# Local transformer: order of the turns and projections within a step

## The reference

```python
def attn_layer(x, Wqkv, qs, ksc, Wo):
    qkv = x @ Wqkv
    q, k, v = (sh(t) for t in jnp.split(qkv, 3, -1))      # 16 heads of 64
    q = l2norm(q) * qs
    k = l2norm(k) * ksc
    q = q * cos * scale + rotate_half(q) * sin * scale
    k = k * cos * inv + rotate_half(k) * sin * inv
    out = local_attention(q, k, v)                         # softmax in windows
    return out.transpose(0, 2, 1, 3).reshape(b, n, INNER) @ Wo
...
for i in range(DEPTH):                                     # DEPTH = 6
    x = attn_layer(shift_tokens(x), Wqkv[i], q_scale[i], k_scale[i], Wo[i]) + x
    x = ffn_layer(shift_tokens(x), ln_g[i], ln_b[i], W1[i], b1[i], W2[i], b2[i]) + x
```

## Time and profile before

| | |
|---|---|
| median of three timed runs | 2600.63 us (2596.15 to 2601.51) |
| the profiled execution | 2589.45 us, span 2587.7 us |
| PE busy | 2448.3 us (95%), 52349 matmuls |
| DVE busy | 2154.9 us (83%) |
| ACT busy | 2033.9 us (79%) |
| POOL busy | 1519.4 us (59%) |

### The profile page before, as it was taken

One profiled execution on the slowest core, in us unless ns is written; L12 is line 12 of the kernel. 1 busy time (PEld: TensorE's weight loads), 2 busy tenths in 40 slices (PEclk: granted clock), 3 DMA queues, 4 the chain that ended last, 5 costly groups with the idle time before them and its releaser, 6 DMA issues. The chain is left out here.

```text
span 2587.7 us, 118567 instructions
## 1 busy us (share of the span) xinstructions
PE 2448.3 (95%) x52349; PEld 1973.1 (76%) x52349; DVE 2154.9 (83%) x2455; ACT 2033.9 (79%) x4077; POOL 1519.4 (59%) x1029
## 2 busy tenths in 40 slices
PE   6799999999999999999999999699999999997999
PEld 2488888888888888888888887467776776775787
DVE  5888888888888888888888886389898988885898
ACT  4689888898889899898998886667676766664776
POOL 3788888888888888887898784122222222222110
PEclk9899999999999999999999999799999999999999
DMA  3234433443444344334443332123232322221221
GB/s 99 56 93 95 108 78 93 94 110 83 97 94 110 83 96 99 95 85 98 103 100 82 86 83 59 45 46 69 45 73 48 67 47 66 51 58 30 83 74 41
DMA packets 275793, 202.01 MB, mean 78 GB/s; under 512 B 117568, under 2 KB 215880, under 8 KB 274248
## 3 DMA queue, kind: packets, MB, share of 16 engines
q1 hardware_dynamic: 275280, 194.42, 31.3%
HBM read 36.96 MB, written 1.11 MB: 15 GB/s over the span
## 5 line engine op out<-in xcount | busy, mean ns | idle before, releaser
L514 POOL TENSOR_TENSOR lt_t_sin<-lt_qk,lt_tab 128x512 f32<-128x512 f32 x384 | 683.3, 1801 | 222.2 <-DVE lt_qk L1298 220.1
L519 POOL TENSOR_TENSOR lt_qr<-lt_qr,lt_t_sin 128x1024 f32<-128x1024 f32 x192 | 457.7, 2384 | 28.2 <-POOL lt_t_sin L514 0.9
L2082 DVE TENSOR_REDUCE fa_neg_max<-bank 128x1 f32<-128x1024 f32 x256 | 301.6, 1220 | 91.2 <-PE bank L1879 89.7
L2004 ACT ACTIVATE fa_prob<-bank,fa_neg_max 128x1024 f32<-128x1024 f32 x128 | 142.6, 1114 | 216.5 <-DVE fa_neg_max L2082 164.2
L1905 PE MATMUL bank<-fa_prob_t,fa_v 32*64 32x128 f32 x16384 | 293.6, 276 | 16.5 <-issue 11.8
L1905 PEld LDWEIGHTS bank<-fa_prob_t,fa_v 32*64 32x64 f32 x16384 | 244.4, 130 | 78.0 <-issue 58.1
L2092 DVE STREAM_TRANSPOSE fa_prob_t<-fa_prob 128x1024 f32<-128x1024 f32 x256 | 302.1, 1219 | 0.0
L607 PE MATMUL bank<-lt_w_high,lt_x_high 128*128 128x512 f32 x576 | 262.3, 455 | 0.8 <-ACT lt_v_tok L1011 0.4
L979 ACT COPY lt_qk<-bank 128x512 f32<-128x512 f32 x384 | 224.3, 589 | 23.7 <-PE bank L609 2.8
L1298 DVE TENSOR_TENSOR lt_qk<-lt_qk,lt_rn 128x2048 f32<-128x2048 f32 x96 | 239.8, 2498 | 2.4 <-ACT lt_rn L1005 2.2
L1291 DVE TENSOR_REDUCE lt_ssq<-lt_qr 128x32 f32<-128x2048 f32 x96 | 218.9, 2280 | 25.6 <-ACT lt_qr L987 25.6
(11 more groups left out here) (260 smaller groups left out, 5853.1 us busy)
## 6 DMA issues: line engine op xcount, KB each, us to landing
lt_v<-lt_v_tok SPq DMA_DIRECT2D x576, 128.0 KB
fa_v<-fa_v_tok SPq DMA_DIRECT2D x256, 128.0 KB, 2.7
lt_v<-lt_v_tok SPq DMA_DIRECT2D x192, 64.0 KB
lt_k_t<-lt_k_t SPq DMA_DIRECT2D x84, 128.0 KB, 2.9
lt_v<-lt_v SPq DMA_DIRECT2D x168, 64.0 KB, 2.0
lt_w_raw<-in_lt_wqkv_dram SPq DMA_DIRECT2D x36, 256.0 KB, 3.6
ex_cw_all<-cw_kept SPq DMA_DIRECT2D x8, 1024.0 KB, 4.6
lt_x_s<-h_in SPq DMA_DIRECT2D x96, 64.0 KB, 2.7
```

What stands on the lines that cost most here:

```text
L514: pool.tensor_tensor(dst[:, :, i, :], src[:, :, 1 - i, :], tab[:, g // 2 % 2, 1, at:at + 32].unsqueeze(1).to_broadcast([P, HEADS, 32]), AL ...
L519: pool.tensor_tensor(qr[:, g % 2, half], qr[:, g % 2, half], t_sin[:, :], ALU.add).then_inc(S.rotated, 1)
L2082: dve.tensor_reduce(neg_max[:, u % 2, par:par + 1], bank[:, 2 * par:2 * par + 2, :].rearrange("p a n -> p (a n)"), AX.X, ALU.max, negate=T ...
```

## The change

On TensorE, and in the same way in the order of the banks and in ScalarE's emptying:

- before: query turns (j 0, 1), two projections, key turns (j 2, 3), two projections, variance (odd steps), attention's turn, scores;
- after: query turns, variance (odd steps), attention's turn, key turns, four projections, scores.

```diff
@@ order of the banks
                 for j in (2 * a, 2 * a + 1):
                     if live(i):
                         uses["turn", i, j] = len(uses)
-                for j in (2 * a, 2 * a + 1):
-                    if live(i + 2):
-                        uses["qk", i + 2, j] = len(uses)
-            if live(i - 2):
-                uses["att", i - 2, 0] = len(uses)
-                uses["att", i - 2, 1] = len(uses)
+                if live(i - 2) and a == 0:
+                    uses["att", i - 2, 0] = len(uses)
+                    uses["att", i - 2, 1] = len(uses)
+            for j in range(4):
+                if live(i + 2):
+                    uses["qk", i + 2, j] = len(uses)
@@ TensorE
                         for j in (2 * a, 2 * a + 1):
                             if live(i):
                                 turn_qk(i, j)
-                        for j in (2 * a, 2 * a + 1):
-                            if live(i + 2):
-                                project_qk(i + 2, j)
-                        if i == 0 and a == 0:
+                        if live(i - 2) and a == 0:
+                            if even(i, 5) is not None:
+                                variance(even(i, 5))
+                            turn_att(i - 2, 0)
+                            turn_att(i - 2, 1)
+                    if even(i, 5) is not None and not live(i - 2):
+                        variance(even(i, 5))
+                    for j in range(4):
+                        if live(i + 2):
+                            project_qk(i + 2, j)
+                        if i == 0 and j == 1:
                             second_var(3)
-                    if even(i, 5) is not None:
-                        variance(even(i, 5))
-                    if live(i - 2):
-                        turn_att(i - 2, 0)
-                        turn_att(i - 2, 1)
@@ ScalarE
                         for j in (2 * a, 2 * a + 1):
                             if live(i):
                                 empty_turned(i, j)
-                        for j in (2 * a, 2 * a + 1):
-                            if live(i + 2):
-                                empty_qk(i + 2, j)
-                        if i == 0 and a == 0:
+                        if live(i - 2) and a == 0:
+                            empty_att(i - 2, 0)
+                            empty_att(i - 2, 1)
+                    for j in range(4):
+                        if live(i + 2):
+                            empty_qk(i + 2, j)
+                        if i == 0 and j == 1:
                             second_log(3)
                             second_rstd(3)
-                    if live(i - 2):
-                        empty_att(i - 2, 0)
-                        empty_att(i - 2, 1)
```

## The result

The changed kernel takes 2612.86 us (median of 7 runs, 2608.98 to 2619.65). The kernel before, run beside it, takes 2597.98 us (7 runs, 2595.04 to 2601.51). The ratio is 1.006 [1.0048, 1.0073]: slower by 14.9 us.

The account below looks back on a forecast made before the run. TensorE's own instruction stream was taken to set the step length in the local transformer. The terms 11.3 + 6.9 - 3.5 = 14.7 gave +15 us, so 2616 us, range 2600 to 2628.

Parts of the forecast that it names:

- The reordering itself at nothing: TensorE in the local transformer: no instruction added or removed, a block costs the same wherever it stands; cost 0.
- the lead-in: Extra time before the mask matmul, now behind a projection: 0.10 us a step kept, bounds 0 and 0.20.
- "faster" rival: Before the mask and scores: lead-in (9.3 us) and late instructions (13) both go, giving -4, so 2596; chance 0.10.
- Part 1, down step: Attention's turn waits for VectorE's second norm_att half; scores 0.31 us late, 0.24 a step on average, 47 steps: 11.3 us.
- The guess for steps without the split: Down steps without ScalarE's weight split (0.52 us): exponent still comes last, barely; where not, the whole 0.31 us counts.
- Part 2, up step: Variance waits 0.10 us for ScalarE's square; scores 0.14 late, nothing absorbs it; 46 x 0.15 = 6.9 us.
- Banks: Four rotating banks emptied by ScalarE's copies in time for turns and projections; tightest margin 0.4 us, cost nil.
- Part 3, late instructions: Fewer late instructions in the scores: 3.5 us off 8.4 us of standing matmuls; bounds 0 and -13.
- the rule of proportion: Ahead of the scores, six matmuls instead of ten cross 4 in 10 fewer packet boundaries, hence 3.5 us off.
- the clock: Longer transpose runs drop TensorE's clock for the twelve projections behind: 12 x 0.24 x 93 = 268, so 2884; chance 0.03.
- "Nothing": VectorE and ScalarE run ahead once TensorE is slower, the waits close: 2601, within 0.2%; chance 0.05.
- The draw by supply: Slow projections ahead of the scores relieve late instructions by 13 us instead of 3.5: +5, so 2606; chance 0.20.

Follow-up runs that it names:

- `down_only`: New order in even (down) steps alone, old order in odd ones, against the kernel before: 2608.64 us, ratio 1.0042.
- `swap_after`: Whole new order, plus both halves of VectorE's norm_att ahead of the residual in odd steps, against the kernel before: 2593.35 us, ratio 0.9978.
- `up_only`: New order in odd (up) steps alone, old order in even ones, against the kernel before: 2600.09 us, ratio 1.0009.
- `mid`: Attention's turn and variance moved only ahead of the second pair of projections, against the kernel before: 2587.33 us, ratio 0.9953.
- `both_after`: `swap_after` plus TensorE's centring ahead of weigh_v and ScalarE's square earlier in even steps, against the kernel before: 2597.2 us, ratio 0.999.
- `fill_old`: New order only from step 4 on, old order in the steps that fill the pipeline, against the kernel before: 2610.0 us, ratio 1.0036.

## Why the prediction was right

The forecast was 2616.0 for a median of 2612.86, and +15 for +14.9 us. The agreement of the sum is closer than that of its terms.

**The reordering itself at nothing, and the lead-in.** Right. The last L609 starts at 737.06 and the mask at 737.38: 0.32 where projections are 0.23 apart, so the lead-in of about 0.10 stays behind a projection. With it half of the "faster" rival falls. The late instructions, its other half, came out at -7.5 and could not pay for the waits alone.

**Part 1, down step.** Right in mechanism and size, by its own signs: L692 waits for VectorE 46 times, starts at 1.15 (1.13 in the working), the scores are 0.33 late (0.31), the probabilities' turn 0.23 (0.22). The step grew by 0.23, 0.23 and 0.19 in the three pairs of old and new order, in the mean 0.22 instead of 0.24: 10.3 us for 11.3. The guess for steps without the split held too: they grew from about 14.9 to 15.16, those with it from 15.38 to 15.61. `down_only` shows the loss with this part alone (+10.5), and `swap_after` takes the wait away and the loss with it.

**Part 2, up step.** Right in mechanism: the variance stands 0.10. The scores are 0.20 late instead of 0.14, since the variance took 0.54 to the next block (748.12 to 748.66) and not 0.42 as in the earlier trace rows. The step grew by 0.15, 0.11 and 0.09, in the mean 0.12: 5.5 us for 6.9. By time alone this part isn't shown (`up_only`, +1.9, interval across nothing); its step length and its row of waits show it.

**Banks.** Right: no wait of L692 or L607 for ScalarE's copies is among the rows. TensorE's one wait of that kind is the mask's for `lt_k_t`, 0.8 us in one place.

**Part 3, late instructions.** The direction was right and the size too small: -7.5 us (-6.5 over all kernels) against -3.5, well inside its bounds of 0 and -13. The step that failed is the rule of proportion, by which six matmuls ahead instead of ten cross 4 in 10 fewer boundaries. Four fifths of the standing went, not two fifths. By the Trainium skill, "Runtime: NRT & Kernel Launch", section "Instruction fetch mechanics", where crossings are mostly hidden, this term would be 0. Most crossings are hidden here too: 244 packets came in the 1440 us of before, and 12 holes stood in its scores. But those that aren't hidden cost 9.3 us before and 1.8 after, so the term isn't 0. `mid` has only two of the four projections there and 2.6 us, so the third and fourth add little. Why so much goes was not found.

**What the prediction left out: the fill.** It looked at the steady steps alone. In the first steps GpSimd is late and projections are the only work that can be done meanwhile; the new order puts them behind the wait. Price 4.5 us at the first scores, roughly 1.7 once the pipeline is full.

**The account.** Counted from the first rotation, the last mask comes after 1510.8, 1515.6 and 1515.6 us in before and its repeats, and after 1527.6, 1527.3 and 1526.9 in after and its repeats: 13.3 more in the mean. From the 18th mask to the last, 78 steps, it is +7.4: steps 39 x 0.22 + 39 x 0.12 = 13.3, late instructions -7.5 x 78 / 93 = -6.3, together 7.0. Up to the 18th it is +5.9: the fill 1.7, and steps 13 x 0.17 = 2.2; 2 us there are not assigned. The remaining 1.6 us of the 14.9 lie outside the local transformer or in the scatter. So the sum of the prediction was right partly by luck. Its own terms, as measured, make 10.3 + 5.5 - 7.5 = 8.3: 2.4 us too much in the steps and 4 too little relief in the scores were offset by 6.6 us that the prediction did not have; 1.7 of them are the fill, and most of the rest is not explained.

**The rivals.** From 160 us on the clock stayed at 1.00 with 24 transposes behind one another in down steps (in up steps the variance stands between them, which the prediction's factor of 93 passed over), so that rival falls, and the rule of "TensorE: Matmul & The Clock Gate", section "Part 4: PE-mode transpose", in the Trainium skill does not show in the time there. In the fill the clock did fall, behind idle stretches and with either order. "Nothing" falls: VectorE could not run ahead. The draw by supply was nearest to being right in its mechanism, but 7.5 us of relief was short of the 13 that it needed.

## What to carry to other kernels

When a block is moved forward on the bounding engine, write down for each of its inputs when the producer ends, and whether that producer hangs on the bounding engine's own last instruction; if it does, the wait is locked in and stays in every step. Such a wait can be removed on the producer's side, by doing the wanted half first (`swap_after`), or by moving the block half as far (`mid`); here both came out faster than before. But the block that is moved instead may itself be a cover for another wait (`both_after`). And count times in a fill from an event that the change can't touch, not from the program's start, or a later start hides a real effect, as it nearly did in `fill_old`. Do it over several profiles, since single ones differ by as much as what is looked for.

## What the runs showed of the hardware

Whether small matmuls run out of instructions depends on what stands right ahead of them, more than on how many instructions the program has or where its packets end: 9.3 us of holes in the scores with the attention's turn and the mask ahead, 1.8 with four projections and the mask, and moving all instructions by 128 left both much as they were (10.7 and 1.9), though it moved the holes to other steps. Each of the twelve holes of before ended 2.2 to 3.2 us after the start of an instruction packet. The cause of so large a step was not found.

In down steps 24 transposes stood behind one another (731.53 to 734.40, a wait of 0.3 us among them), in up steps 8 and 16 with the variance's two matmuls between them; over some 90 steps the granted clock stayed at 1.00.

The time at which the local transformer's first rotation starts differs between kernels whose code up to there does the same, from 80.8 to 86.4 us. This is a range of 5.6 us in single profiled executions, a third of what was to be explained here. Two profiles of the same instructions differ by 1.3 to 1.4 us there (80.8 and 82.2, 81.7 and 83.1).
